# Moving the first job of the shared banks ahead of the keys in every slot of a one-core attention block

## The chip, the core and the metric

The kernel runs on one core of a Trainium2 chip. What counts is the device time of one execution, in microseconds (us). Three runs of the kernel before took 1745.03, 1745.07 and 1747.44 us; their median is 1745.07 us. One more execution was profiled, and all rows in this document come from it. The engines are named as in the profile: PE is TensorE (matmuls), PEld its weight loads, DVE VectorE, ACT ScalarE, POOL GpSimd, SP the engine that issues the DMAs.

## The reference, cut to what is computed

The batch is 32 sequences of 64 positions with width 512. Attention has 32 heads of width 128; a mask and a bias for each head and batch are added to the scores.

```python
xn  = layernorm(x)
q   = xn  @ Wq                 # (32*64, 32 heads, 128)
k   = ctx @ Wk ; v = ctx @ Wv
s   = q k^T * 128**-0.5 + bias # per batch and head, 64 x 64
p   = softmax(where(mask, s, -inf)), masked places 0
x   = x + tanh(g_xattn) * ((p v) @ Wo)
y   = layernorm(x)
x   = x + tanh(g_ffn) * (y @ Wf^T + bias + lora(y, adapter of the batch))
```

Everything is float32. The kernel keeps each matmul operand in two parts, `hi` (the value rounded) and `lo` (what the rounding left), and forms a product from three matmuls: hi·hi, hi·lo, lo·hi.

## The kernel before, in words

**Slots.** The 2048 rows are cut into 4 blocks of 512. A slot is one head of one block, so there are 128 slots, numbered n = 0 to 127; block b holds slots 32b to 32b+31. In a slot PE computes the queries of head n into `q_bank` (12 matmuls, `queries`), the keys into `k_bank` (12, `keys`), two jobs in the shared banks `vo_bank0/1` (`main_job(n, 0)` and `main_job(n, 1)`, 12 matmuls each), the scores of head n into `s_two` (8) and the attention of head n-1 into `pv_two` (8).

**Jobs of the shared banks.** Four heads make a group, and the two jobs of a slot go by n modulo 4. Slots 3 and 0 (modulo 4) compute values for a group (`values`), slots 1 and 2 compute the output projection of a finished group (`output`). The first output job of a group, in slot 1 (modulo 4), waits for `ot_lo`, the lo part of the attention result of the group's last head; that head's attention ran on PE at the end of the slot just before. Some slots carry more behind the two jobs: a `turn` (4 transposes of a normalised tile, in slots 9, 10, 13, 14 of blocks 1 to 3 and 25, 26, 29, 30 of blocks 0 to 2), a LoRA product (15, 16) or a piece of the dense layer (17 to 20, and the last slot of all).

**The other engines.** Each has a written list per slot and works it off in order. After the scores of a head DVE adds the bias and finds `row_max`; POOL subtracts it (`shift`); ACT takes the exponential; DVE sums rows and inverts; POOL scales (`probabilities`); DVE transposes through `pv_two` (`transposes`); ACT rounds to `pt` hi; DVE forms `pt` lo (`rest_of_probabilities`). That serves the attention of the next slot. The attention result goes ACT `attn`, DVE `attn` (the sum), ACT `ot_hi`, POOL `ot_lo`. A key tile goes ACT `kt` (hi), DVE `kt` (lo); a value tile ACT `v_hi`, DVE `v_lo`; an output job is added into `acc` by DVE.

**Weights.** Blocks 1 to 3 read weights back from DRAM already split. In block 0 they are split on the way: ACT makes the hi part (`weights_q`, `weights_vo`, `weights_k`), POOL the lo part of `wq`, `wk` and `wv`, DVE that of `wo` (`weights_o`, one piece before the transposes and one after, in slots 3 and 0 modulo 4). SP saves the split weights and loads the next raw ones, each in list order: in a slot it waits for `wq` lo, then for `wk` lo, then loads the raw pair for `wv` or `wo`.

Lines of the profile that the steps below touch: L296 to L298 are the three matmuls of a product, L301/L302 those of scores and attention, L575 the transposes of a turn, L679 every rounding on ACT, L743 ACT's half of `attn`, L737 `pt` hi, L858 every lo part on DVE, L887 the addition into `acc`, L903/L908 the transposes of the probabilities, L915 `pt` lo, L928/L933 scores and row maximum, L937 the attention sum, L965 the normalised tile, L1112 every lo part on POOL.

Of the kernel before, what the change touches and what calls it, by code (L numbers as in the profile page):

```python
# [163 lines left out]
def flamingo_block(nc, x, ctxt, pair_bias, mask, wq, wk, wv, wo, g_xattn, g_ffn, wf, fbias, lora_a, lora_b,  # L164
                   lora_starts, lora_const, out):
    with ExitStack() as ctx:
# [99 lines left out]
        def parts(pair, *at):  # L266
            return [p[at] for p in pair]
# [198 lines left out]
        def _(pe):  # L466
            def queries(n):
                b = n // H
                if n % H == 0:
                    pe.wait_ge(vo_free, NUMBER["turn", LEAD, b, PB - 1] + 1)  # L470
                if n < H:
                    pe.wait_ge(wq_lo, n + 1)
                else:
                    pe.wait_ge(wq_back, 16 * (n - H + 1))
                wait(pe, q_lo, n)
                for c in range(C):
                    mm = mm3(pe, q_bank[:, :], parts(q_w, slice(None), c, slice(None)),
                             parts(xt[b % 2], slice(None), c, slice(None)), c == 0, c == C - 1)
                mm.then_inc(q_ps, 1)

            def keys(n):
                b = n // H
                if n < H:
                    pe.wait_ge(wk_lo, n + 1)
                else:
                    pe.wait_ge(wk_back, 16 * (n - H + 1))
                wait(pe, k_lo, n)
                for c in range(C):
                    mm = mm3(pe, k_bank[:, :], parts(k_w, slice(None), c, slice(None)),
                             parts(ct[b % 2], slice(None), c, slice(None)), c == 0, c == C - 1)  # L490
                mm.then_inc(k_ps, 1)
# [53 lines left out]
            def main_job(n, k):  # L545
                if values_at(n):
                    g, tiles = values_at(n)
                    values(g, tiles[k])
                elif output_at(n):
                    g, tiles = output_at(n)  # L550
                    output(g, tiles[k])
# [55 lines left out]

            def slot(n):
                queries(n)
                keys(n)  # L610
                main_job(n, 0)
                main_job(n, 1)
                if turn_at(n):
                    turn(*turn_at(n))
                if lora_at(n):
                    lora_inner(*lora_at(n))
                if dense_at(n):
                    dense(*dense_at(n))
                scores(n)
                attention(n - 1)  # L620
# [56 lines left out]
        def _(act):  # L677
# [36 lines left out]
            def keys(n):  # L714
                wait(act, s_ps, n)
                act.wait_ge(k_ps, n + 1)
                hi(k_part(0), by(k_bank, PB), k_hi)
# [7 lines left out]
            def main_job(n, k):  # L725
                if values_at(n):
                    g, tiles = values_at(n)
                    values(g, tiles[k])

            def probabilities(n):  # L730
                if n == 0:
                    act.wait_ge(pt_zero, PB)
                wait(act, pv_ps, n)
                act.wait_ge(turn_done, n + 1)
                for r in range(2):
                    rows = cols(r, S)
                    last = act.activation(pt[rows, :, 0, rows], turned[rows, :, :], ACT.Copy)  # L737
                last.then_inc(pt_hi, 1)
# [40 lines left out]
            def slot(n):  # L779
                if n > 0:  # L780
                    queries(n)
                if n + 1 < H:
                    weights_q(n + 1)
                weights_vo(n)
                if n > 0:
                    keys(n)
                if n + 1 < H:
                    weights_k(n + 1)
                if n > 0:
                    probabilities(n - 1)  # L790
                if piece_at(n):
                    piece(n)
                if n > 0:
                    main_job(n, 0)
                    main_job(n, 1)
                if turn_at(n):
                    turn(*turn_at(n))
                if lora_at(n):
                    lora(*lora_at(n))
                if n > 0:  # L800
                    attention_half(n - 1)
                exps(n)
                if n > 0:
                    attention(n - 1)
# [51 lines left out]
        def _(dve):  # L856
# [7 lines left out]
            def keys(n):  # L864
                dve.wait_ge(k_hi, n + 1)
                lo(k_part(1), by(k_bank, PB), k_part(0), k_lo)
# [31 lines left out]
            def transposes(n):  # L898

                if n == 0:  # L900
                    dve.wait_ge(vo_free, NUMBER["v", 0, PB - 1] + 1)
                dve.wait_ge(prob_done, n + 1)
                dve.transpose(turned[:, :, :], prob[:, :, :]).then_inc(square_done, 1)  # L903
                dve.wait_ge(square_done, n + 1)
                for a in range(2):
                    for i in range(2):
                        of, to = cols(2 * a + i, S // 2), cols(2 * a + 1 - i, S // 2)
                        last = dve.transpose(turned[to, :, cols(i, S // 2)], prob[of, :, cols(1 - i, S // 2)])  # L908
                last.then_inc(turn_done, 1)

            def rest_of_probabilities(n):
                dve.wait_ge(pt_hi, n + 1)
                for r in range(2):
                    rows = cols(r, S)
                    last = dve.tensor_tensor(pt[rows, :, 1, rows], turned[rows, :, :], f32(pt[rows, :, 0, rows]),  # L915
                                             ALU.subtract)
                last.then_inc(pt_lo, 1)
# [102 lines left out]
            def slot(n):  # L1020
                if n > 0:
                    queries(n)
                    weights_o(n, 0)
                    transposes(n - 1)
                    keys(n)
                    rest_of_probabilities(n - 1)
                    weights_o(n, 1)
                if sums_at(n):
                    statistics(*sums_at(n))
                if turn_at(n):  # L1030
                    normalise(*turn_at(n))
                if n > 0:
                    main_job(n, 0)
                    main_job(n, 1)
                if turn_at(n):
                    turn(*turn_at(n))
                if lora_at(n):
                    lora_gate(*lora_at(n))
                if dense_at(n):
                    dense(*dense_at(n))  # L1040
                scores(n)
                if n > 0:
                    attention(n - 1)
                if lora_at(n):
                    lora_rest(*lora_at(n))
                row_scales(n)
                if n in CONSTANTS:
                    constants(CONSTANTS.index(n))
# [221 lines left out]
```

## Time and profile before

| | |
|---|---|
| median of three runs | 1745.07 us |
| the profiled execution | 1747.61 us, its span 1745.8 us |
| PE busy | 1726.5 us of the span, in 8666 matmuls |
| DVE, ACT, POOL busy | 1232.4, 619.3, 613.6 us |
| granted TensorE clock, mean | 0.997 |
| DMA | 336.50 MB, mean 193 GB/s; 281 to 215 GB/s in block 0, mostly 160 to 200 later |

The span is one execution from the first to the last instruction; 1.8 us of the execution lie outside it. PE's busy time is above 90% in all but the first and last of 40 slices, so the order of PE's own list sets the time, and another engine matters only where PE waits for it.

### The profile page before, as it was taken

Reading aid. Unit: us, or ns where it says so; the run is one execution under the profiler, and the core shown is the slowest. Engines: PE = TensorE matmul, PEld = TensorE weight load, DVE = VectorE, ACT = ScalarE, POOL = GpSimd, SP = SyncE. Lnnn points to the kernel's source line nnn. Section 1 sums busy time; section 2 is a strip of 40 time slices with the busy share of each in tenths; the row PEclk is TensorE's granted clock in tenths of the full one; section 3 lists DMA queues with packets and bytes.
Section 4 is the critical chain, followed back from the end, with each engine's and each line's share of the span. In section 5 each row is a group of like instructions: output and inputs, shape, how many; then the busy total and the mean of one; then the engine's idle time right before and its main releaser. Section 6 shows DMA issues by size and latency. Waiting matters only on the chain.

```text
span 1745.8 us, 25078 instructions
## 1 busy us (share of the span) xinstructions
PE 1726.5 (99%) x8666; PEld 1464.7 (84%) x8666; DVE 1232.4 (71%) x2649; ACT 619.3 (35%) x1225; POOL 613.6 (35%) x811
## 2 busy tenths in 40 slices
PE   8999999999999999999999999999999999999998
PEld 6888888888888888888888888888888888888887
DVE  6788777877777765667767776567766777666674
ACT  4544444454333332233333333223333333333321
POOL 4656666554232321233233232223332322222221
PEclk9999999999999999999999999999999999999999
DMA  7777777766545444555445454355455454454431
GB/s 281 266 260 257 280 262 273 279 233 215 183 169 199 170 163 159 192 174 200 163 167 195 167 193 171 134 200 192 164 184 178 170 197 159 159 193 162 177 125 49
DMA packets 111456, 336.50 MB, mean 193 GB/s; under 512 B 13361, under 2 KB 13489, under 8 KB 111330
## 3 DMA queue, kind: packets, MB, share of 16 engines
q1 hardware_dynamic: 111186, 334.63, 54.2%
q8 instruction: 70, 1.15, 0.3%
q14 instruction: 56, 0.46, 0.1%
q10 hardware_dynamic: 144, 0.26, 0.1%
HBM read 263.54 MB, written 71.30 MB: 192 GB/s over the span
## 4 chain that ended last, share of the span: by engine, by line
PE 95%; DVE 1%; issue 1%; POOL 1%; DMA 1%; ACT 0%; SPq 0%; ACTq 0%; DVEq 0%
PE vo_bank L296 13%; PE vo_bank L298 13%; PE vo_bank L297 13%; PE q_bank L296 7%; PE q_bank L298 7%; PE q_bank L297 7%; PE k_bank L296 6%; PE k_bank L297 6%; PE k_bank L298 6%; PE pv_two L301 5%; PE s_two L301 5%; PE pv_two L302 2%; PE s_two L302 2%; PE vo_bank L575 1%; DMA acc<-in_wv 0%
## 5 line engine op out<-in xcount | busy, mean ns | idle before, releaser
L1169 POOL TENSOR_TENSOR score<-score,row_max 128x256 f32<-128x256 f32 x128 | 78.8, 616 | 813.5 <-DVE row_max L933 813.5
L1112 POOL TENSOR_TENSOR ot_lo<-attn,ot_hi 128x512 fp32r<-128x512 f32 x128 | 165.7, 1294 | 151.5 <-ACT ot_hi L679 151.5
L296 PE MATMUL q_bank<-xt_hi,wq 128*128 128x512 f32 x512 | 209.0, 408 | 0.0
L298 PE MATMUL q_bank<-xt_hi,wq 128*128 128x512 f32 x512 | 201.0, 393 | 0.0
L297 PE MATMUL q_bank<-xt_lo,wq 128*128 128x512 f32 x512 | 200.4, 391 | 0.0
L296 PE MATMUL k_bank<-ct_hi,wk 128*128 128x512 f32 x512 | 199.3, 389 | 0.5 <-DVE ct_lo L858 0.5
L298 PE MATMUL k_bank<-ct_hi,wk 128*128 128x512 f32 x512 | 199.2, 389 | 0.0
L297 PE MATMUL k_bank<-ct_lo,wk 128*128 128x512 f32 x512 | 199.2, 389 | 0.0
L296 PE MATMUL vo_bank<-wv,ct_hi 128*128 128x512 f32 x504 | 196.3, 390 | 0.3 <-POOL wv L1112 0.3
L297 PE MATMUL vo_bank<-wv,ct_hi 128*128 128x512 f32 x504 | 196.1, 389 | 0.0
L298 PE MATMUL vo_bank<-wv,ct_lo 128*128 128x512 f32 x504 | 196.1, 389 | 0.0
L296 PE MATMUL vo_bank<-wo,ot_hi 128*128 128x512 f32 x496 | 193.2, 390 | 0.3 <-POOL ot_lo L1112 0.2
L298 PE MATMUL vo_bank<-wo,ot_lo 128*128 128x512 f32 x496 | 193.1, 389 | 0.0
L297 PE MATMUL vo_bank<-wo,ot_hi 128*128 128x512 f32 x496 | 193.0, 389 | 0.0
L743 ACT ACTIVATE attn<-pv_two 128x512 f32<-128x512 f32 x128 | 76.7, 599 | 318.8 <-PE pv_two L302 318.8
L908 DVE STREAM_TRANSPOSE pv_two<-prob 32x128 f32<-32x128 f32 x512 | 165.3, 323 | 9.6
L737 ACT ACTIVATE pt<-pv_two 64x256 fp32r<-64x256 f32 x256 | 97.0, 379 | 161.6 <-DVE pv_two L908 160.1
L858 DVE TENSOR_TENSOR v_lo<-vo_bank,v_hi 128x512 fp32r<-128x512 f32 x126 | 86.4, 691 | 89.4 <-ACT v_hi L679 88.1
L903 DVE STREAM_TRANSPOSE pv_two<-prob 128x256 f32<-128x256 f32 x128 | 58.9, 460 | 119.0 <-POOL prob L1183 118.7
L679 ACT ACTIVATE kt<-k_bank 128x512 fp32r<-128x512 f32 x128 | 76.6, 598 | 181.1 <-PE k_bank L298 180.4
L301 PE MATMUL s_two<-kt,qt_hi 128*128 128x256 f32 x512 | 127.8, 327 | 5.6 <-issue 5.6
L301 PE MATMUL pv_two<-pt,v_hi 128*128 128x256 f32 x512 | 132.9, 337 | 0.2 <-issue 0.2
(200 smaller groups left out, 3748.1 us busy)
## 6 DMA issues: line engine op xcount, KB each, us to landing
wv<-wv_split SPq DMA_DIRECT2D x96, 512.0 KB, 5.3
wq<-wq_split SPq DMA_DIRECT2D x96, 512.0 KB, 3.2
wk<-wk_split SPq DMA_DIRECT2D x96, 512.0 KB, 3.6
wo<-wo_split SPq DMA_DIRECT2D x96, 512.0 KB, 5.2
raw_bias<-in_pair_bias SPq DMA_DIRECT2D x64, 256.0 KB, 5.8
wq_split<-wq SPq DMA_DIRECT2D x32, 512.0 KB, 2.9
wk_split<-wk SPq DMA_DIRECT2D x32, 512.0 KB, 4.1
wv_split<-wv SPq DMA_DIRECT2D x32, 512.0 KB, 5.9
```

Source lines behind the costliest of these rows:

```text
L296: pe.matmul(to, left[0], right[0], start=first, stop=False)
L297: pe.matmul(to, left[0], right[1], start=False, stop=False)
L298: return pe.matmul(to, left[1], right[0], start=False, stop=last)
L301: pe.matmul(to, left[0], right, start=True, stop=False)
L302: return pe.matmul(to[:, 0, :], left[1], right[:, 0], start=False, stop=True)
L679: act.activation(to, src, func).then_inc(done, 1)
L737: last = act.activation(pt[rows, :, 0, rows], turned[rows, :, :], ACT.Copy)
L743: act.activation(by(attn, PB), pv_two[:, :, 1, :], ACT.Copy).then_inc(ot_b, 1)
L858: dve.tensor_tensor(to, src, f32(of), ALU.subtract).then_inc(done, 1)
L908: last = dve.transpose(turned[to, :, cols(i, S // 2)], prob[of, :, cols(1 - i, S // 2)])
L1112: pool.tensor_tensor(to, src, f32(of), ALU.subtract).then_inc(done, 1)
L1169: pool.tensor_tensor(score[:, :, :], score[:, :, :], row_max[:, :].unsqueeze(2).to_broadcast([P, PB, S]), ALU.subtract).then_inc(shift_don ...
```

## The change

Three lists are reordered; no instruction is added or removed. PE's slot becomes queries, first job, keys, second job, extras, scores, attention. ACT's list takes `probabilities` (the `pt` rounding) and the first job before `keys`; in block 0 the rounding of `wk` still follows `keys`. DVE's list takes `rest_of_probabilities`, the first job and the second piece of `weights_o` before `keys`. POOL's and SP's lists are as they were.

```diff
@@ PE
             def slot(n):
                 queries(n)
+                main_job(n, 0)
                 keys(n)
-                main_job(n, 0)
                 main_job(n, 1)
@@ ACT
                 weights_vo(n)
                 if n > 0:
+                    probabilities(n - 1)
+                    main_job(n, 0)
                     keys(n)
                 if n + 1 < H:
                     weights_k(n + 1)
-                if n > 0:
-                    probabilities(n - 1)
                 if piece_at(n):
                     piece(n)
                 if n > 0:
-                    main_job(n, 0)
                     main_job(n, 1)
@@ DVE
                     queries(n)
                     weights_o(n, 0)
                     transposes(n - 1)
+                    rest_of_probabilities(n - 1)
+                    main_job(n, 0)
+                    weights_o(n, 1)
                     keys(n)
-                    rest_of_probabilities(n - 1)
-                    weights_o(n, 1)
                 if sums_at(n):
                     statistics(*sums_at(n))
                 if turn_at(n):
                     normalise(*turn_at(n))
                 if n > 0:
-                    main_job(n, 0)
                     main_job(n, 1)
```

PE in slot 61 (block 1, 61 is 1 modulo 4, an output slot with a turn), before; of each product only rows that wait stand here:

```order
L296 MATMUL q_bank<-xt1_hi,wq 128x512 [waits q_lo,wq_back]
...
L296 MATMUL k_bank<-ct1_hi,wk 128x512 [waits k_lo,wk_back]
...
L296 MATMUL vo_bank0<-wo,ot1_hi 128x512 [waits vo_free,wo_back,ot_lo]
...
L296 MATMUL vo_bank1<-wo,ot1_hi 128x512 [waits vo_free]
...
L575 MATMUL vo_bank0<-ident,xn0 128x128 [waits vo_free,xn_done]
...
L301 MATMUL s_two<-kt,qt_hi 128x256 [waits score_done,k_lo,q_lo]
```

And the same rows now:

```order
L296 MATMUL q_bank<-xt1_hi,wq 128x512 [waits q_lo,wq_back]
...
L296 MATMUL vo_bank0<-wo,ot1_hi 128x512 [waits vo_free,wo_back,ot_lo]
...
L296 MATMUL k_bank<-ct1_hi,wk 128x512 [waits k_lo,wk_back]
...
L296 MATMUL vo_bank1<-wo,ot1_hi 128x512 [waits vo_free]
...
L575 MATMUL vo_bank0<-ident,xn0 128x128 [waits vo_free,xn_done]
...
L301 MATMUL s_two<-kt,qt_hi 128x256 [waits score_done,k_lo,q_lo]
```

The product that waits for `ot_lo` moved up by the 12 matmuls of the keys; the keys moved down by the 12 matmuls of that product.

DVE in slot 12 (block 0, 0 modulo 4, a value slot in which a second piece of `wo` is split), before, from the transposes on:

```order
L903 STREAM_TRANSPOSE pv_two<-prob 128x256 [waits prob_done]
L908 STREAM_TRANSPOSE pv_two<-prob 32x4x32 [waits square_done]
L908 STREAM_TRANSPOSE pv_two<-prob 32x4x32 x3
L858 TENSOR_TENSOR kt<-k_bank,kt 128x4x128 [waits k_hi]
L915 TENSOR_TENSOR pt<-pv_two,pt 64x4x64 [waits pt_hi]
L915 TENSOR_TENSOR pt<-pv_two,pt 64x4x64
L858 TENSOR_TENSOR wo<-raw_vo,wo 128x512 [waits wo_hi]
L858 TENSOR_TENSOR v_lo<-vo_bank,v_hi 128x2x256 [waits vo_hi] x2
```

And now (line numbers one lower, since the file is a line shorter):

```order
L902 STREAM_TRANSPOSE pv_two<-prob 128x256 [waits prob_done]
L907 STREAM_TRANSPOSE pv_two<-prob 32x4x32 [waits square_done]
L907 STREAM_TRANSPOSE pv_two<-prob 32x4x32 x3
L914 TENSOR_TENSOR pt<-pv_two,pt 64x4x64 [waits pt_hi]
L914 TENSOR_TENSOR pt<-pv_two,pt 64x4x64
L857 TENSOR_TENSOR v_lo<-vo_bank,v_hi 128x2x256 [waits vo_hi]
L857 TENSOR_TENSOR wo<-raw_vo,wo 128x512 [waits wo_hi]
L857 TENSOR_TENSOR kt<-k_bank,kt 128x4x128 [waits k_hi]
L857 TENSOR_TENSOR v_lo<-vo_bank,v_hi 128x2x256 [waits vo_hi]
```

`kt` lo, for which the scores wait, moved from before `pt` lo to behind `pt` lo, the first value tile and the piece of `wo`. In blocks 1 to 3 the row of `wo` is not there.

ACT in the same slot, before:

```order
L679 ACTIVATE wo<-raw_vo 128x512 [waits vo_ps,raw_vo_in1,wo_saved]
L679 ACTIVATE kt<-k_bank 128x4x128 [waits k_ps,s_ps]
L679 ACTIVATE wk<-raw_k 128x512 [waits wk_saved,k_ps,raw_k_in]
L737 ACTIVATE pt<-pv_two 64x4x64 [waits turn_done,pv_ps]
L737 ACTIVATE pt<-pv_two 64x4x64
L679 ACTIVATE v_hi<-vo_bank 128x2x256 [waits vo_ps,pv_ps] x2
```

And now:

```order
L679 ACTIVATE wo<-raw_vo 128x512 [waits vo_ps,raw_vo_in1,wo_saved]
L737 ACTIVATE pt<-pv_two 64x4x64 [waits turn_done,pv_ps]
L737 ACTIVATE pt<-pv_two 64x4x64
L679 ACTIVATE v_hi<-vo_bank 128x2x256 [waits vo_ps,pv_ps]
L679 ACTIVATE kt<-k_bank 128x4x128 [waits k_ps,s_ps]
L679 ACTIVATE wk<-raw_k 128x512 [waits wk_saved,k_ps,raw_k_in]
L679 ACTIVATE v_hi<-vo_bank 128x2x256 [waits vo_ps,pv_ps]
```

The roundings of `kt` and `wk` moved behind that of `pt` and of the first value tile.

## Rows read from the trace of the kernel before

**Rows 1.** Waits of PE: waited for, total us, times, longest us.
```profile
PE s_two L301 <- issue: 5.6, 2, 4.1
PE vo_bank L575 <- DVE acc L887: 4.4, 3, 1.9
```

**Rows 2.** Timeline of PE, slots 60 and 61: start us, us, instruction.
```profile
805.99 0.45 PE L296 MATMUL q_bank<-xt_hi,wq 128*128 128x512 f32 x1
...
816.95 0.28 PE L301 MATMUL s_two<-kt,qt_hi 128*128 128x256 f32 x1
...
818.75 0.45 PE L296 MATMUL q_bank<-xt_hi,wq 128*128 128x512 f32 x1
...
821.55 0.39 PE L296 MATMUL k_bank<-ct_hi,wk 128*128 128x512 f32 x1
...
824.27 0.39 PE L296 MATMUL vo_bank<-wo,ot_hi 128*128 128x512 f32 x1
```

**Rows 3.** Timeline of DVE, ACT and POOL from those scores to `ot_lo`.
```profile
817.84 0.69 DVE L858 TENSOR_TENSOR v_lo<-vo_bank,v_hi 128x512 fp32r<-128x512 f32 x1 [1.28 <-ACT v_hi L679]
...
820.67 0.69 DVE L937 TENSOR_TENSOR attn<-pv_two,attn 128x512 f32<-128x512 f32 x1
...
821.75 0.62 ACT L679 ACTIVATE ot_hi<-attn 128x512 fp32r<-128x512 f32 x1
...
822.45 1.29 POOL L1112 TENSOR_TENSOR ot_lo<-attn,ot_hi 128x512 fp32r<-128x512 f32 x1 [1.11 <-ACT ot_hi L679]
```

**Rows 4.** Timeline of POOL and PE, slot 25: its first output job.
```profile
336.53 1.30 POOL L1112 TENSOR_TENSOR ot_lo<-attn,ot_hi 128x512 fp32r<-128x512 f32 x1 [1.39 <-ACT ot_hi L679]
...
337.89 0.50 PE L296 MATMUL vo_bank<-wo,ot_hi 128*128 128x512 f32 x1 [0.19 <-POOL ot_lo L1112]
```

**Rows 5.** Timeline of DVE, slot 60: `kt` and `pt` lo.
```profile
813.72 0.69 DVE L858 TENSOR_TENSOR kt<-k_bank,kt 128x512 fp32r<-128x512 f32 x1
...
814.59 0.86 DVE L915 TENSOR_TENSOR pt<-pv_two,pt 64x256 fp32r<-64x256 f32 x2 [0.17 <-ACT pt L737]
```

**Rows 6.** Timeline of DVE and PE, slot 58, an output slot with a turn.
```profile
788.59 0.86 DVE L915 TENSOR_TENSOR pt<-pv_two,pt 64x256 fp32r<-64x256 f32 x2 [0.17 <-ACT pt L737]
789.48 0.55 DVE L965 TENSOR_SCALAR xn<-acc,mean_var,rstd 128x512 f32<-128x512 f32 x1
...
791.00 0.60 PE L575 MATMUL vo_bank<-ident,xn 128*128 128x128 f32 x4
```

**Rows 7.** Timeline of DVE and PE, slot 12 in block 0.
```profile
175.23 0.86 DVE L915 TENSOR_TENSOR pt<-pv_two,pt 64x256 fp32r<-64x256 f32 x2 [0.17 <-ACT pt L737]
...
176.12 0.69 DVE L858 TENSOR_TENSOR wo<-raw_vo,wo 128x512 fp32r<-128x512 f32 x1
...
177.09 0.28 PE L301 MATMUL s_two<-kt,qt_hi 128*128 128x256 f32 x1
```

**Rows 8.** Timeline of DVE and PE at the start (slot 1) and the end (slot 127).
```profile
37.65 0.86 DVE L915 TENSOR_TENSOR pt<-pv_two,pt 64x256 fp32r<-64x256 f32 x2 [0.48 <-ACT pt L737]
...
37.26 0.55 PE L301 MATMUL s_two<-kt,qt_hi 128*128 128x256 f32 x1 [4.05 <-issue]
...
1696.40 0.86 DVE L915 TENSOR_TENSOR pt<-pv_two,pt 64x256 fp32r<-64x256 f32 x2 [0.17 <-ACT pt L737]
...
1697.04 0.28 PE L301 MATMUL s_two<-kt,qt_hi 128*128 128x256 f32 x1
```

**Rows 9.** Timeline of PE and DVE around the turns of slots 25 and 57.
```profile
345.52 0.63 PE L575 MATMUL vo_bank<-ident,xn 128*128 128x128 f32 x4 [1.90 <-DVE acc L887]
...
774.91 1.29 DVE L952 BATCH_NORM_STATS2 stats<-acc 128x6 f32<-128x512 f32 x2
...
776.39 0.52 DVE L965 TENSOR_SCALAR xn<-acc,mean_var,rstd 128x512 f32<-128x512 f32 x1
...
777.78 0.63 PE L575 MATMUL vo_bank<-ident,xn 128*128 128x128 f32 x4 [1.23 <-DVE acc L887]
```

**Rows 10.** Windows of PE: stretch, length, PE busy (matmuls), granted clock, DMA, GB/s.
```profile
775.00:778.00 3.00, 1.77 (x9) 1.00 0.74 295
...
346.70:350.00 3.30, 3.30 (x15) 0.50 0.99 385
```

## The prediction

> **What bounds the kernel now.** I read the page first: PE is busy in nearly every slice, so its own list sets the time. The waits of PE come next [rows 1]: two waits before scores at the start (5.6 us) and three before turns (4.4 us) are nearly all. The timeline of a plain slot then gives the floor [rows 2]: queries begin at 805.99 and the next ones at 818.75, so a slot takes 12.76 us of unbroken PE work; queries are 2.80 us (818.75 to 821.55), 12 matmuls of keys or of a job 2.72 us (821.55 to 824.27). A reordering takes none of this away. It can gain only from the 10 us of waits, and it can lose wherever a product moves ahead of its operand. So each wait in PE's list has to be asked how late its operand comes. All times below are those of the profiled execution, 1747.61 us (span 1745.8 and 1.8 outside); the median of the runs lies 2.5 us lower.
>
> **The first output job of a group.** In 31 slots (5, 9, ... 125) the first job waits for `ot_lo` of the head whose attention PE finished just before the slot. In slot 61 the scores before it began at 816.95 [rows 2]; from there DVE sums at 820.67, ACT rounds at 821.75, POOL works 822.45 to 823.74 [rows 3]. That is 6.79 us after the scores. The job began 7.32 us after them (824.27), so 0.53 us was spare. In slot 25, where the chain was late, PE already waited, and began at 337.89, 0.06 us after POOL's end at 337.83 [rows 4]. The job now begins behind the queries alone: 821.55, 4.60 us after the scores, but `ot_lo` lets it go at 6.79 + 0.06 = 6.85. PE stands still 2.25 us, with the keys, the second job and the scores queued behind it. Nothing of this comes back, for neither DVE, ACT nor POOL can start that chain sooner: its parts hang on the scores and attention of the slot before.
>
> The chain is not the same everywhere. In front of it DVE has the second value tile of slot 60 (817.84 for 0.69 us, [rows 3]), which delays the scores' sums by 0.32 us. Where slot n-1 has a long PE tail (after LoRA and dense work: 49, 53, 81, 85, 113) that tile is done early and the wait is 1.93 us; the same holds in block 0, for a reason below. Blocks 1 to 3: 17 x 2.25 + 5 x 1.93 = 47.9 us, and slots 57 and 89 apart. There PE waits today before the turn, since DVE runs statistics and normalisation (774.91 to 776.91, [rows 9]) before the addition that frees the bank. The first job's bank is now freed before; but `kt` lo, which stands ahead of the statistics, comes late, as the keys end 6.85 + 5.44 + 0.17 = 12.46 us after the scores of slot 56. ACT's rounding (0.6) and DVE's (0.6 until the next can start) bring the statistics to 13.7, their 2.0 us and a hand-over of 0.1 the turn to 15.8, where it began 14.2 after those scores: 1.6 us each, 3.2 together. Sum 51.1.
>
> Block 0: five slots at 1.93 = 9.7, and slots 25 and 29, which already wait, 1.7 together. Sum 11.4.
>
> **The scores' wait for `kt` lo.** DVE used to form `kt` lo (813.72) while ACT rounded `pt`, so it cost nothing; then `pt` lo to 815.45 [rows 5], 1.50 us before the scores at 816.95. Now the value tile or addition (0.60 until the next may start) and `kt` lo (0.69) follow `pt` lo, with gaps of 0.03 and a hand-over of 0.10: 1.42 us. That is 0.08 less than the 1.50 there are: a plain slot costs nothing, but the cover is nearly gone. Bounds: 0 and, if the pieces run 0.13 longer each, 0.2 us in 24 slots, 5 us.
>
> In slots with a turn that are 2 modulo 4 (12 of them) the normalised tile also comes behind `kt` lo: 789.45 + 0.03 + 0.60 + 0.60 + 0.55 + 0.10 = 791.33 for a turn that began at 791.00 [rows 6]: 0.33 x 12 = 4.0 us. Those that are 1 modulo 4 are covered by the longer slot.
>
> In block 0, slots 0 and 3 modulo 4 also have a piece of `wo` (0.73) between. Slot 12: `pt` lo ends 176.09 [rows 7], less 0.32 (PE waited in slot 11 too, so the second value tile is out of the way before the scores; that is the reason named above), + 0.03 + 0.60 + 0.73 + 0.69 + 0.10 = 177.92 against scores at 177.09: 0.83 us. Other slots of the eight stand at 0.8 to 1.6; I take 1.05: 8.4 us. Slots 3 modulo 4 (seven from 7 on) come out at 0.85 to 1.6 by the same sum, and their raw `wo` arrives later, since SP asks for it only after POOL's `wk` and `wv` lo, which follow the keys' rounding on ACT. Bounds of that: 0, where the chain has other reasons to be late, and the 2.7 us by which the keys move; I take 0.4, near the lower end, as ACT needs the load only before it rounds `pt`: 7 x 1.4 = 9.8 us.
>
> Start: in slot 1 the scores wait for `kt` lo as it is (37.26), `pt` lo ending at 38.51 [rows 8]; with `pt` first, both scores waits grow by about 1, and slot 3 has two pieces of `wo` and a late load: 4.4 us in all, between 1 and 8. End: slot 127 has no job; `pt` lo ends at 1697.26, + 0.03 + 0.69 + 0.10 = 1698.08 against 1697.04 [rows 8]: 1.0 us.
>
> Sum without the clock: 51.1 + 11.4 + 4.0 + 8.4 + 9.8 + 4.4 + 1.0 = 90.1 us.
>
> **The clock.** After the 1.90 us of idle PE before the turn of slot 25 [rows 9] the granted clock fell to 0.50, that is 1.2 in place of 2.4 GHz, for about 3.4 us [rows 10], which costs half, 1.7 us. After 1.23 us idle in slot 57 [rows 9] it stayed at 1.00 [rows 10]. The 31 new waits leave PE idle 1.8 to 2.1 us (the wait less 0.17 us in which the last matmul drains), as long as the one after which it fell; but that one was followed by transposes and short matmuls, these by full ones. Bounds: none of them, 0, and all, 53 us. I take half of them, 15.5 x 1.7 = 26 us.
>
> The Trainium skill (TensorE: Matmul & The Clock Gate, section "HAM oscillation — how this bites in real kernels") has as its rule that only idle gaps longer than any of these let the clock fall. By that rule the 26 us would be 0. The trace does not agree: it fell after 1.90 us [rows 9, 10].
>
> Forecast: 1747.6 + 90.1 + 26 = 1863.7 for a profiled execution, 1861 for a run.
>
> **Rivals.**
> The clock holds in all new waits (the page's rule above would have it so): 1745.1 + 90.1 = 1835. For it: two of three waits near a turn left the clock alone. Against it: [rows 10].
> The clock falls in all of them: 1835 + 53 = 1888. For it: a fall after a shorter idle time. Against it: full matmuls before and after.
> The starved block 0: SP's later loads put ACT's rounding of `wo` ahead of `pt` by 2 us more in 14 slots, 28 us on top: 1889. Against it: ACT has nothing else to do between the queries' rounding and `pt`, so the load must be over 2 us late before it counts.
> The other side, not slower, is that the bank relief decides. Place: turns of slots 25, 57 and 89, where the addition that frees the bank now stands before the statistics. Price: the 4.4 us of waits [rows 1] and one spell at half clock, 1.7, so 1739. It decides only if the wait for `ot_lo` stays below 6 / 31 = 0.2 us, so only if POOL's part ended 4.7 us after the scores and not 6.79. Nothing in the rows shortens that chain by 2 us.
> The change not doing what it says is excluded by the order: the waiting product stands ahead of the keys.
>
> **How the numbers follow.** Some falls of the clock, 1848 to 1878: 0.45. No falls, 1825 to 1848: 0.25. All falls or the starved block, 1878 to 1905: 0.20. A smaller loss than any of these, 1750 to 1825 (half of the waits hidden by something I don't see): 0.05. Not slower, 1739: 0.03, and within 0.2%: 0.02. A change of 0.2% (3.5 us) is about what a measurement of this kernel can tell from none. Range 1825 to 1895: it leaves out 0.10 below and some 0.05 above.
>
> **What would show it.** Right: PE's waits have a new first line, the output job at L296 behind POOL's `ot_lo`, about 31 times and near 60 us; in a slot like 61 the job begins 6.85 us after the scores; scores wait in block 0 alone, 14 to 17 times and near 1 us; some 15 spells at clock 0.50 each behind such a wait; plain slots 60, 62 and 63 still take 12.76 us. Wrong: `ot_lo` ending earlier than 6.4 us after the scores, waits for `kt` in every slot of blocks 1 to 3, or a block 0 that grows by more than 50 us.

## The result and the profile after

The changed kernel takes 1853.11 us (median of four runs, 1848.67 to 1858.37); the kernel before, run beside it, takes 1745.05 (1744.06 to 1747.44). The ratio is 1.0613, with a 95% interval of 1.0599 to 1.0627: slower by 108 us. The forecast was 1861, range 1825 to 1895. The profiled execution spans 1846.8 us against 1745.8, 101.0 us more and not 108: it took 1848.67 us, the least of the four, and the profiled one of before took 1747.61, more than any of its four.

The page shows the same instructions in a longer span. First the busy times of the engines, then the chain that ended last:

```profile
PE 1753.6 (95%) x8666; PEld 1466.0 (79%) x8666; DVE 1217.3 (66%) x2649; ACT 612.1 (33%) x1225; POOL 617.5 (33%) x811
...
PE 80%; DVE 8%; POOL 4%; issue 4%; ACT 3%; DMA 1%; SPq 0%; ACTq 0%; DVEq 0%
```

PE was busy 99% and made up 95% of the chain; now it stands still for 5% of the span, and the chain leaves it for DVE, ACT and POOL. Its waits (waited for, total us, times, longest us), against [rows 1]:

```profile
PE vo_bank L296 <- POOL ot_lo L1111: 59.2, 31, 2.1
PE s_two L301 <- issue: 20.3, 18, 3.7
PE vo_bank L575 <- DVE xn L964: 3.4, 6, 1.4
```

The new first line is the output job behind POOL's `ot_lo`, in all 31 groups. The scores' waits grew from 5.6 us in 2 to 20.3 in 18 ("issue" stands there for `kt` lo, as the timelines below show): slots 1 and 2, the slots 0 and 3 modulo 4 from 3 to 32 but 31, and 127. The turn's wait for an addition on DVE is gone, but one for the normalised tile `xn` has come in its place, 1.4 us in slot 25 and 0.66 in 57 and 89, so little of it is won.

Slot 61 on PE, with the scores of slot 60 ahead of it (start us, us, instruction, idle time and releaser); it answers to [rows 2]:

```profile
867.77 0.28 PE L301 MATMUL s_two<-kt,qt_hi 128*128 128x256 f32 x1
...
874.58 0.50 PE L296 MATMUL vo_bank<-wo,ot_hi 128*128 128x512 f32 x1 [2.02 <-POOL ot_lo L1111]
874.92 0.40 PE L297 MATMUL vo_bank<-wo,ot_hi 128*128 128x512 f32 x1
...
877.48 0.39 PE L296 MATMUL k_bank<-ct_hi,wk 128*128 128x512 f32 x1
```

And the chain on DVE, ACT and POOL in that stretch, as in [rows 3]:

```profile
868.66 0.69 DVE L857 TENSOR_TENSOR v_lo<-vo_bank,v_hi 128x512 fp32r<-128x512 f32 x1 [1.08 <-ACT v_hi L679]
...
871.49 0.69 DVE L936 TENSOR_TENSOR attn<-pv_two,attn 128x512 f32<-128x512 f32 x1
...
872.57 0.61 ACT L679 ACTIVATE ot_hi<-attn 128x512 fp32r<-128x512 f32 x1
...
873.26 1.27 POOL L1111 TENSOR_TENSOR ot_lo<-attn,ot_hi 128x512 fp32r<-128x512 f32 x1 [1.11 <-ACT ot_hi L679]
```

The chain is as long as before: `ot_lo` ends at 874.53, 6.76 us after the scores (6.79 before). The queries end 4.6 us after them, and PE goes on at 874.58, 6.81 after them; 6.85 was forecast. One thing was not: the second matmul of the job starts 0.34 us after the first, where matmuls in a row follow at 0.23 (0.31 to 0.34 over the 31 waits), so each such wait costs 0.1 us on top of the idle time.

Where each part of a period (scores to scores) changed, after less before, read slot by slot from the two traces:

| group of slots | forecast | measured |
| --- | --- | --- |
| 1 modulo 4, blocks 1 to 3 (24), without the clock | 51.1 | 53.4 |
| 1 modulo 4, block 0 (7) | 11.4 | 13.8 |
| 2 modulo 4 with a turn (12) | 4.0 | 3.6 |
| 0 modulo 4, slots 4 to 32 (8) | 8.4 | 7.1 |
| 3 modulo 4 from slot 7 on, block 0 (7) | 9.8 | 9.2 |
| up to the scores of slot 3 | 4.4 | 2.1 |
| slot 127 | 1.0 | 1.05 |
| half-clock spells behind the new waits | 26 | 11.4 |
| slot 26: a half-clock spell of before is gone | - | -1.1 |
| all others | 0 | 0.4 |
| sum | 116 | 101.0 |

One entry has another cause than the rest of its row. In slot 31 PE waits not for `kt` lo but for the DMA that brings `wv` back, since the first job, which needs it, comes sooner (neither the kernel before nor that of experiment 10, with the old order in this slot, has the wait):

```profile
PE vo_bank L296 <- DMA wv<-wv_split: 1.3, 1, 1.3
```

### The profile page after: what moved, and what is told of

Its sections match the earlier page's. It is cut to its first block, busy times and chain, and to the rows that moved or that the text cites. A ratio compares the mean times of both kernels' runs of the same rounds, so it can differ in the third digit from the quotient of the medians.

```text
span 1846.8 us, 25078 instructions
## 1 busy us (share of the span) xinstructions
PE 1753.6 (95%) x8666; PEld 1466.0 (79%) x8666; DVE 1217.3 (66%) x2649; ACT 612.1 (33%) x1225; POOL 617.5 (33%) x811
## 4 chain that ended last, share of the span: by engine, by line
PE 80%; DVE 8%; POOL 4%; issue 4%; ACT 3%; DMA 1%; SPq 0%; ACTq 0%; DVEq 0%
PE vo_bank L296 13%; PE vo_bank L297 12%; PE vo_bank L298 12%; PE k_bank L296 6%; PE k_bank L297 6%; PE k_bank L298 6%; PE q_bank L296 5%; PE q_bank L298 5%; PE q_bank L297 5%; PE s_two L301 4%; DVE score L927 4%; PE pv_two L301 3%; POOL ot_lo L1111 2%; ACT ot_hi L679 2%; PE s_two L302 1%
## 5 line engine op out<-in xcount | busy, mean ns | idle before, releaser
L296 PE MATMUL vo_bank<-wo,ot_hi 128*128 128x512 f32 x496 | 201.0, 405 | 59.2 <-POOL ot_lo L1111 59.2
L297 PE MATMUL vo_bank<-wo,ot_hi 128*128 128x512 f32 x496 | 197.9, 399 | 0.0
L298 PE MATMUL vo_bank<-wo,ot_lo 128*128 128x512 f32 x496 | 197.5, 398 | 0.0
L914 DVE TENSOR_TENSOR pt<-pv_two,pt 64x256 fp32r<-64x256 f32 x256 | 108.1, 422 | 116.6 <-ACT pt L737 114.9
L296 PEld LDWEIGHTS vo_bank<-wo,ot_hi 128*128 128x128 f32 x496 | 95.2, 192 | 91.8 <-POOL ot_lo L1111 72.3
L301 PE MATMUL s_two<-kt,qt_hi 128*128 128x256 f32 x512 | 128.7, 329 | 20.3 <-issue 20.3
```

The lines of the kernel that those rows point to most:

```text
L296: pe.matmul(to, left[0], right[0], start=first, stop=False)
L297: pe.matmul(to, left[0], right[1], start=False, stop=False)
L298: return pe.matmul(to, left[1], right[0], start=False, stop=last)
L301: pe.matmul(to, left[0], right, start=True, stop=False)
```

## The experiments

All twelve are built from the two kernels. Ratios are against the kernel before, run beside them on the same chip (medians 1747.6, 1748.2 and 1746.8 us), with 95% intervals. "A spell" is a stretch in which full matmuls follow each other at 0.43 us in place of 0.23.

**1. Old order in the slots with the waits.** The changed kernel with the order of before in slots 1 modulo 4, on PE, ACT and DVE. The edit on PE (ACT and DVE alike):

```diff
 queries(n)
-main_job(n, 0)
-keys(n)
+if n % G == 1:
+    keys(n); main_job(n, 0)
+else:
+    main_job(n, 0); keys(n)
```

> The changed kernel, with the old order (keys before the first job) put back on PE, ACT and DVE in the slots that are 1 modulo 4 alone. Theory (the attention result's lo part is late): all 31 waits for ot_lo go, 53 us of them in blocks 1 to 3, 14 in block 0 and the 11 us of half clock behind them, so 1853 - 78 = 1775 us. Rival (the new order costs in every slot, through kt lo or the banks, and the wait on ot_lo only shows it): the time then moves into the other slots, and stays above 1820 us.

Measured: 1771.96 us, ratio 1.0151 (1.0125 to 1.0177); the forecast of 1775 held, the rival (over 1820) did not. In its profile the slots 1 modulo 4 of blocks 1 to 3 are within 0.1 us of before in sum, and no spell is left but those at the start, up to slot 3. What remains is block 0 (6.9 us in slots 0 modulo 4, 7.7 in slots 3 modulo 4), the turns of slots 2 modulo 4 (3.7), the start and the end. So of the 108 us, 84 go when the 31 slots are put back (80 by the two profiles), and 24 stay.

**2 and 3. The wait, pushed back.** In the changed kernel the first output job waits for the last head's `ot_lo` only ahead of that head's three matmuls (2), or after the first head's three (3), its first matmuls needing only the earlier heads:

```diff
-pe.wait_ge(ot_lo, G * (g + 1))
+pe.wait_ge(ot_lo, G * (g + 1) - 1)
 ...
-output_heads(g, t, range(G))
+output_heads(g, t, range(3))       # range(1) in the other kernel
+pe.wait_ge(ot_lo, G * (g + 1))
+output_heads(g, t, range(3, G))    # range(1, G)
```

> The changed kernel, with the first output job's wait split: its first three heads (9 of 12 matmuls) wait only for the heads before, the last three matmuls for ot_lo of the last head. Theory: 9 x 0.2265 = 2.04 of each wait of 2.25 us are filled with work, 31 x 2.04 = 63 us and the 11 us of half clock go, some 4 us come back as waits before turns: about 1783 us. Rival (the keys behind the job are what is late, or the banks): nothing is gained by splitting, 1853 us.

> As the split after three heads, but after one: 3 x 0.2265 = 0.68 us of each wait filled, idle time per wait about 1.4 us in place of 2.1. Theory for the waits: 31 x 0.68 = 21 us less. For the clock: if falls hang on the length of the idle time, there are none behind these waits and another 11 us go: 1821 us. Rival: the clock falls as often as before, 7 times: 1832 us.

Measured: 1779.54 us, ratio 1.019 (1.0169 to 1.021), for the first, where 1783 was forecast: the wait is gone, no output job is followed by a spell, and 74 of the 108 us are saved. The second: 1819.26 us, ratio 1.0418 (1.0398 to 1.0438). Its wait of PE:

```profile
PE vo_bank L296 <- POOL ot_lo L1116: 37.5, 31, 1.4
```

Thirty-one waits are there still, 1.0 to 1.4 us each, and none of them is followed by a spell. The forecast of 1821 held, its rival of 1832 (spells as before) did not. So it is not enough for a spell that there is such a wait; among these waits its length matters.

**4. The new PE order only where the wait is.** The kernel before, with PE's first job ahead of the keys in slots 1 modulo 4; ACT and DVE as before:

```diff
 queries(n)
+if n % G == 1:
+    main_job(n, 0)
 keys(n)
-main_job(n, 0)
+if n % G != 1:
+    main_job(n, 0)
 main_job(n, 1)
```

> The kernel before, with the new order in the slots that are 1 modulo 4 on PE alone; ACT's and DVE's lists are the old ones everywhere. Theory: the 31 waits for ot_lo are there, 53 + 12 us, with some falls of the clock (0 to 15 us), and nothing of block 0's waits for kt lo: 1745 + 65 + 8 = 1818 us. Rival (loss spread over all slots): under 1775 us.

Measured: 1866.33 us, ratio 1.0687 (1.0668 to 1.0707). The forecast missed by 48 us. Its waits of PE:

```profile
PE vo_bank L296 <- POOL ot_lo L1115: 63.9, 31, 2.9
PE vo_bank L575 <- DVE acc L890: 17.6, 12, 3.5
```

The second line has grown from 4.4 us in 3 before: 12 turns wait for the addition that frees their bank. And 18 of the 31 waits are followed by a spell, where the changed kernel has 7. Block 0's slots 0 and 3 modulo 4 are as before, as expected.

**5. The piece of `wo` behind the keys on DVE.** The changed kernel, block 0:

```diff
 main_job(n, 0)
-weights_o(n, 1)
 keys(n)
+weights_o(n, 1)
```

> The changed kernel, with the second piece of wo (block 0, slots 0 and 3 modulo 4) behind the keys on DVE in place of before them. Theory: each of the 15 waits for kt lo in block 0 gets 0.73 us shorter, 11 us: 1842 us. Rival (they wait for SP's late raw weights or ACT): no change, 1853 us.

Measured: 1855.28 us, ratio 1.0611 (1.0588 to 1.0634), as the changed kernel; 1842 was forecast, a miss. First slot 12 in the changed kernel, which answers to [rows 7], then in this one (DVE, POOL and PE in both):

```profile
186.67 0.86 DVE L914 TENSOR_TENSOR pt<-pv_two,pt 64x256 fp32r<-64x256 f32 x2 [0.90 <-ACT pt L737]
...
188.17 0.68 DVE L857 TENSOR_TENSOR wo<-raw_vo,wo 128x512 fp32r<-128x512 f32 x1
188.34 1.64 POOL L1111 TENSOR_TENSOR wk<-raw_k,wk 128x512 fp32r<-128x512 f32 x1 [2.50 <-ACT wk L679]
188.76 0.68 DVE L857 TENSOR_TENSOR kt<-k_bank,kt 128x512 fp32r<-128x512 f32 x1
189.55 0.36 PE L301 MATMUL s_two<-kt,qt_hi 128*128 128x256 f32 x1 [0.50 <-issue]
...
192.57 0.42 DVE L932 TENSOR_REDUCE row_max<-score 128x4 f32<-128x256 f32 x1
```

```profile
187.65 0.68 DVE L857 TENSOR_TENSOR kt<-k_bank,kt 128x512 fp32r<-128x512 f32 x1
187.83 1.27 POOL L1111 TENSOR_TENSOR wk<-raw_k,wk 128x512 fp32r<-128x512 f32 x1 [2.49 <-ACT wk L679]
188.25 1.40 DVE L857 TENSOR_TENSOR wo<-raw_vo,wo 128x512 fp32r<-128x512 f32 x1
188.43 0.36 PE L301 MATMUL s_two<-kt,qt_hi 128*128 128x256 f32 x1 [0.43 <-issue]
189.57 0.68 DVE L857 TENSOR_TENSOR v_lo<-vo_bank,v_hi 128x512 fp32r<-128x512 f32 x1
...
191.94 0.42 DVE L932 TENSOR_REDUCE row_max<-score 128x4 f32<-128x256 f32 x1
```

The first shows the forecast's order: `pt` lo, value tile, `wo`, `kt` lo, and the scores 0.11 us behind `kt` lo. In the second `kt` lo no longer stands behind `wo`, yet the scores' wait is shorter by 0.07 only. `wo` now delays the work behind it: `row_max` starts 3.51 us after the scores in place of 3.02.

The two profiles show where the forecast 11 us went. The fifteen waits of the scores got shorter, but by 3.6 us in sum. The seven waits for `ot_lo` of block 0 got longer by 3.1 us in sum (about 2.2 us each in place of 1.7), and those of slots 9, 21 and 25 are now followed by a spell, where none was. That the later `row_max` is what makes these waits longer, and keeps the scores' waits from shrinking by the full 0.73 us each, is likely, since an item moved along DVE's list stands in the way of another there, but no run shows it by itself.

`wo` took 1.40 us here, and 0.68 in the changed kernel, though POOL works on `wk` beside it in both. What differs is who began. Here POOL did (187.83): it took 1.27 us, and `wo` ended 0.55 us after it (188.25 + 1.40 against 187.83 + 1.27). In the changed kernel `wo` began 0.17 us ahead of POOL, and it was POOL that took longer, 1.64 us. With POOL idle `wo` took 0.69 us in all 12 such cases of the kernel before. The value tile and `kt`, which DVE reads from PSUM on one side, kept their 0.68 or 0.69 beside POOL. This agrees with the Trainium skill (SBUF — State Buffer, section "Who interferes with whom"), by which a DVE instruction with both inputs in SBUF contends with a POOL instruction that reads SBUF, over a port pair that only one of them can hold.

**6 and 7. PE's list alone.** The kernel before with PE's new order in all slots and the old lists on ACT and DVE; and the same with the wait pushed back as in 2:

```diff
 queries(n)
-keys(n)
 main_job(n, 0)
+keys(n)
 main_job(n, 1)
```

> PE's list as in the changed kernel, ACT's and DVE's as before (kt ahead of pt). Theory: kt lo then waits only for the keys themselves, which end 10.2 us after the scores, and is ready at 11.5, 1.2 us before the next scores; block 0's 17 us of waits for kt lo go, those for ot_lo stay: 1853 - 17 = 1836 us. pt lo then ends at 12.5, 1 us before the attention. Rival (the lists have to match, since pt and the first job now wait behind kt on ACT and DVE): slower than 1853 us.

> PE's list as in the changed kernel with the split after three heads, ACT's and DVE's lists as before. Theory: both late operands are covered; left are 31 x 0.2, some 5 us of waits before turns and the start: 1745 + 6 + 5 + 3 = 1759 us. Rival (the new order has no cost but these, and takes the bank waits of slots 25, 57 and 89 away): 1742 us.

Measured: 1896.99 us, ratio 1.0858 (1.0843 to 1.0873), and 1812.05 us, ratio 1.0364 (1.035 to 1.0378). Both forecasts (1836, 1759) missed. For 6 the rival was right (the lists have to match: slower than 1853); for 7 its rival, 1742, was further off than the forecast. The waits of PE in the first, then ACT, DVE and PE at the turn of slot 61:

```profile
PE vo_bank L296 <- POOL ot_lo L1112: 70.0, 31, 4.5
PE vo_bank L575 <- DVE acc L887: 31.0, 24, 3.5
```

```profile
910.86 0.60 ACT L679 ACTIVATE kt<-k_bank 128x512 fp32r<-128x512 f32 x1 [8.35 <-PE k_bank L298]
...
911.49 0.69 DVE L858 TENSOR_TENSOR kt<-k_bank,kt 128x512 fp32r<-128x512 f32 x1 [5.42 <-ACT kt L679]
912.14 0.86 DVE L915 TENSOR_TENSOR pt<-pv_two,pt 64x256 fp32r<-64x256 f32 x2
913.03 0.55 DVE L965 TENSOR_SCALAR xn<-acc,mean_var,rstd 128x512 f32<-128x512 f32 x1
913.61 1.29 DVE L887 TENSOR_TENSOR acc<-vo_bank,acc 128x512 f32<-128x512 f32 x2
914.45 0.63 PE L575 MATMUL vo_bank<-ident,xn 128*128 128x128 f32 x4 [0.97 <-DVE acc L887]
```

ACT and DVE wait for keys that PE now computes last (8.35 and 5.42 us idle), while the first job, long done, stands behind `kt`, `pt` and `xn`. Its addition starts at 913.61 and holds the bank until 914.3; the turn waits 0.97 us. This is a wait that the changed lists of ACT and DVE save, and the reason of the 17.6 us in 4 as well: there too only PE's list had changed. It is not the whole of the 44 us between 6 and the changed kernel. The waits for `ot_lo` are 11 us longer (70.0 against 59.2) and 19 of them are followed by a spell in place of 7, while the scores wait 16 us less (3.9 against 20.3).

**8. A cheaper start of three turns.** The kernel before; on DVE, where statistics and a turn meet (slots 25, 57, 89), the normalised tile and the first addition go ahead of the statistics:

```diff
-if sums_at(n): statistics(*sums_at(n))
+both_here = bool(sums_at(n) and turn_at(n))
+if sums_at(n) and not both_here: statistics(*sums_at(n))
 if turn_at(n): normalise(*turn_at(n))
-if n > 0: main_job(n, 0); main_job(n, 1)
+if n > 0: main_job(n, 0)
+if both_here: statistics(*sums_at(n))
+if n > 0: main_job(n, 1)
```

> The kernel before, where a slot has both statistics and a turn (25, 57, 89): DVE takes the normalised tile and the first job's addition ahead of the statistics, which serve a later tile. PE's list is the old one. Theory: the three waits before these turns (1.90, 1.23, 1.23 us idle) and the one spell at half clock (1.7 us) go, 0.6 us come back by the later scores: 1745 - 5.5 = 1739.5 us, ratio 0.997. Rival (the turn then waits for the tile, the scores for DVE): within 1 us of 1745.

Measured: 1744.12 us in 9 runs against 1748.2 in 13, ratio 0.9975 (0.9965 to 0.9985): faster than both kernels, by 4.1 us against the kernel before where 5.5 were forecast. The periods of slots 57 and 89 are 1.42 us shorter, that of 25 by 1.3, the spell behind it is gone (0.65 us in slot 26), and slots 58 and 90 give back 0.4 each. The turn of slot 57 on DVE and PE, against [rows 9]:

```profile
775.14 0.55 DVE L965 TENSOR_SCALAR xn<-acc,mean_var,rstd 128x512 f32<-128x512 f32 x1
775.72 0.69 DVE L887 TENSOR_TENSOR acc<-vo_bank,acc 128x512 f32<-128x512 f32 x1
776.33 1.28 DVE L952 BATCH_NORM_STATS2 stats<-acc 128x6 f32<-128x512 f32 x2
776.62 0.60 PE L575 MATMUL vo_bank<-ident,xn 128*128 128x128 f32 x4
```

The bank is free at 776.4, ahead of PE, and the 1.23 us of idle time are gone.

**9. The same, with the keys first in slot 1 on ACT.**

```diff
 queries(n)
+if n == 1: keys(n)
 weights_q(n + 1)
+if n == 1: probabilities(0)
 weights_vo(n)
-keys(n)
+if n > 1: keys(n)
 ...
-probabilities(n - 1)
+if n > 1: probabilities(n - 1)
```

> This kernel is e8_before_norm_first (the order of the kernel before, with the normalised tile and the first job ahead of the statistics in slots 25, 57 and 89) with one edit more, on ACT in slot 1 alone: the rounding of the keys and of the probabilities stands ahead of the roundings of the weights of head 2. The trace of before shows the scores of slots 1 to 3 waiting 5.6 us in all for the keys' low part, because the keys' rounding stands behind a whole set of weight roundings. Theory: that ring is what makes PE wait in slot 1, the scores of slot 1 come about 3 us sooner, and since PE then runs without a pause the 3 us stay: about 1741 us, ratio 0.996 or a little less. Rival: the weights of head 2, now rounded some 1.5 us later on ACT and so later on POOL, make the queries or keys of slot 2 wait as long: 1744, same as e8. If the ring is closed elsewhere (DVE), also 1744.

Measured: 1743.77 us in 11 runs, ratio 0.9981 (0.9972 to 0.999). The intervals of 8 and 9 overlap, so no gain over 8 can be told; the rival stands. Slot 1's wait fell from 4.1 us to 1.7, and the scores of slot 2 then waited 2.9 in place of 1.5:

```profile
34.51 0.35 PE L301 MATMUL s_two<-kt,qt_hi 128*128 128x256 f32 x1 [1.69 <-issue]
...
46.74 0.35 PE L301 MATMUL s_two<-kt,qt_hi 128*128 128x256 f32 x1 [2.93 <-issue]
```

Right behind the first of these waits the clock fell to 0.50, after 1.69 us of idle PE. The window (length, PE busy, granted clock, DMA, GB/s):

```profile
35.40:38.50 3.10, 3.05 (x13) 0.50 0.70 232
```

In experiment 8 it fell in slot 2, from 51.8 us on, behind idle times of 1.52 and 0.23 us ahead of the scores and the attention.

**10. The complement of 1.** The kernel before with the new order in slots 1 modulo 4 on all three engines. On PE as in 4; on DVE (ACT likewise):

```diff
 transposes(n - 1)
-keys(n)
-rest_of_probabilities(n - 1)
-weights_o(n, 1)
+if n % G == 1:
+    rest_of_probabilities(n - 1); main_job(n, 0); weights_o(n, 1); keys(n)
+else:
+    keys(n); rest_of_probabilities(n - 1); weights_o(n, 1)
 ...
-if n > 0: main_job(n, 0)
+if n > 0 and n % G != 1: main_job(n, 0)
```

> The order of the kernel before everywhere, except in slots 1 modulo 4, where PE, ACT and DVE all have the new order (first job ahead of the keys). It is the complement of e1 (old order only in those slots, 1772, so 26 us of the 108 were outside them) and differs from e4 (1866) only in that the ACT and DVE lists go along. Theory: the effects are local to a slot; the wait for the attention's low part (24 slots of 2.3 in blocks 1 to 3, 7 of 2.0 in block 0, about 67 us) and the half-clock spells behind it, 11 us, come back, the waits of e4 for the turn's bank do not: 1745 + 53 + 14 + 11 = about 1824, with 5 to 10 spells. Rival: the turns' wait and the more frequent spells of e4 come from the mixture of slots and not from its lists: 1850 or more, some 20 spells. A second rival for the clock alone: 1824 + 15 if some 20 of 31 waits are followed by a spell whatever the lists are.

Measured: 1841.47 us, ratio 1.0537 (1.0518 to 1.0556). The forecast of 1824 fell short by the clock, as its second rival had it:

```profile
PE vo_bank L296 <- POOL ot_lo L1126: 63.9, 31, 2.9
...
PE vo_bank L575 <- DVE acc L894: 0.3, 1, 0.3
```

The wait for `ot_lo` is that of 4 to the last digit, and the turns no longer wait for additions: the 17.6 us of 4 came from the lists that had not been changed. But 17 of the 31 waits are followed by a spell, so the many spells of 4 did not come from there. The other slots of blocks 1 to 3 are within 0.1 us of before in sum. Experiments 1 and 10 add up to 24 + 95 = 119 us for a change that costs 108. The excess of 11 is less than ten more spells at 1.6 us; without spells the slots 1 modulo 4 of blocks 1 to 3 cost 53.6 here and 53.4 in the changed kernel.

**11 and 12. Is a spell chance?** The changed kernel and the kernel of 10, each profiled once more, with no edit.

> The changed kernel itself, profiled a second time, for its half-clock spells alone. In its first profile 7 of the 31 waits for the attention's low part (slots 37, 41, 73, 105, 117, 121, 125) were followed by a spell at half clock. Theory: whether the clock falls behind a wait of about 2 us differs from one execution to the next; then the waits are the same to 0.1 us, but the spells stand behind other slots and their number may be anything from 3 to 12, with the span moving by 1.6 us for each. Rival: the program decides it, by what stands around each wait; then the same seven slots, and a span within 1 us of 1846.8.

> The kernel of e10_new_order_output1_all a second time, again for its spells. There some 17 of 31 waits were followed by one. Theory of chance in each execution: other slots, between 10 and 22 of them. Rival, the program decides: the same slots and a span within 1 us of 1843.6. If both are half right (the mean is the program's, the slots are chance), this one keeps a clearly larger number than the changed kernel in e11, over 12 against under 12.

Measured: spans 1851.3 and 1838.7 us. In 11 the waits followed by a spell are those of slots 37, 41, 73, 105, 117, 121 and 125: the same seven. Experiment 5 shows these seven in blocks 1 to 3 too. In 12 there are 15, of which 14 are among the 17 of experiment 10. So the rival was right nearly throughout as to the slots: the program settles, but for a few, which waits are followed by a spell. It was wrong as to the spans, which it had within 1 us. That of 11 is 4.5 us longer, and 4.4 of that lies ahead of the scores of slot 3: what differs between these executions is the start. That of 12 is 4.9 us shorter, with two spells fewer and 1.0 us less ahead of slot 3's scores.

## Why the forecast held, point by point

**The number.** It came out 8 us above the median of the runs, and 15 above the profiled execution (1863.7 against 1848.67), which is the one that the terms can be held against. The clock's term was 14.6 us too high and the start's 2.3, the waits for `ot_lo` 4.7 too low, and a spell of before that went away (1.1) had no term. The mechanisms were right; that the number came so near is in part these errors working against each other, and the waits and spells below are the better measure. Two signs named ahead were missed: some 15 spells (7), and scores that wait in block 0 alone, 14 to 17 times (18, with slots 32 and 127 among them).

**The bound.** Right. PE's list sets the time, and the slots in which no operand moved (blocks 1 to 3, all but 1 modulo 4 and the turns) changed by 0.4 us in sum over 60 slots (slot 32 stands with block 0, 127 apart).

**The first output job.** Right. The chain kept its length, and 31 waits came out at 59.2 us idle. The term is 64.8 + 13.8 - 11.4 = 67.2 without the clock against 62.5 forecast. The difference is the 0.1 us behind each wait (31 x 0.1 = 3.1), which no row of before had shown apart, and slots 25 and 29, 3.2 us together where 1.7 stood. Slots 57 and 89 came out at 1.8 and 1.6, forecast at 1.6. Experiment 1 shows the cause by taking the order back, experiment 2 by taking only the wait away.

**The scores' wait for `kt` lo.** Right. In plain slots the forecast left 0.08 us of cover; slot 60 took 12.77 us, and here are its `pt`, value and key tiles on DVE, against [rows 5], with the scores at 867.77 right behind:

```profile
865.40 0.86 DVE L914 TENSOR_TENSOR pt<-pv_two,pt 64x256 fp32r<-64x256 f32 x2 [0.90 <-ACT pt L737]
866.29 0.69 DVE L857 TENSOR_TENSOR v_lo<-vo_bank,v_hi 128x512 fp32r<-128x512 f32 x1
866.90 0.68 DVE L857 TENSOR_TENSOR kt<-k_bank,kt 128x512 fp32r<-128x512 f32 x1
```

`kt` ends at 867.58, 0.19 us ahead of the scores, of which 0.11 is the hand-over seen in slot 12: 0.08 spare, as forecast. Slots 2 modulo 4 with a turn grew by 0.31 to 0.35 us each but slot 30, by 0.44 (0.33 forecast); block 0 cost 16.3 against 18.2. The bound of 2.7 us for a late load of `wo` was never reached. The last slot, as in [rows 8]:

```profile
1797.20 0.69 DVE L857 TENSOR_TENSOR kt<-k_bank,kt 128x512 fp32r<-128x512 f32 x1
...
1798.00 0.36 PE L301 MATMUL s_two<-kt,qt_hi 128*128 128x256 f32 x1 [0.89 <-issue]
```

**The start.** Its size can't be judged: 2.1 us in the first profile and 6.5 in the second, where 4.4 was forecast. Two executions of one kernel differ here by as much as the term.

**The clock.** The mechanism is right, the term is the one mis-sized: 11.4 us against 26. Slot 37 on PE, then the windows of its stretches and of the same stretch in slot 61 (length, PE busy, granted clock, DMA, GB/s), against [rows 10]:

```profile
530.56 0.50 PE L296 MATMUL vo_bank<-wo,ot_hi 128*128 128x512 f32 x1 [2.02 <-POOL ot_lo L1111]
530.90 0.39 PE L297 MATMUL vo_bank<-wo,ot_hi 128*128 128x512 f32 x1
...
532.33 0.63 PE L296 MATMUL vo_bank<-wo,ot_hi 128*128 128x512 f32 x1
532.76 0.63 PE L297 MATMUL vo_bank<-wo,ot_hi 128*128 128x512 f32 x1
```

```profile
530.60:531.90 1.30, 1.30 (x5) 0.93 0.41 164
531.95:534.85 2.90, 2.90 (x8) 0.50 0.00 0
...
874.60:878.00 3.40, 3.40 (x15) 1.00 0.19 74
```

After 2.02 us of idle PE the first matmuls still run at full clock, and the fall comes while the fifth runs (from 531.7 us on); then seven or eight follow each other at 0.43 us (1.2 in place of 2.4 GHz), which costs 1.6 us. In slot 61, behind the same 2.02 us, nothing falls. The forecast put one price on all 31 waits, with half of them to fall. But 13 of them were 1.8 us or less (block 0 but slot 25, slots behind a long PE tail, 33 and 89), and the clock fell behind none of these; behind the 18 of 2.0 us and more it fell 7 times. Over the nine profiles here with such waits (two of them second executions of a kernel), 0 of 90 waits for `ot_lo` of 1.8 us or less were followed by a spell, and 95 of 166 of 2.0 us or more. That is no bound for other waits: ahead of scores the clock fell behind 1.69 us (experiment 9). With the count of long waits and the forecast's own half the term would have been 9 x 1.6 = 14. Which long waits are followed by a spell is settled by the program but for a few (experiments 11 and 12); what in it settles that stays open. In blocks 1 to 3 the changed kernel has 7 of 17, that of experiment 10 has 11 of 19, with the same order in these slots and idle times that differ by 0.03 us.

The rule of the Trainium skill that the forecast weighed (TensorE: Matmul & The Clock Gate, section "HAM oscillation — how this bites in real kernels") would have let no such wait count. The runs do not agree: seven spells stand behind some 2.0 us of idle time in the changed kernel.

**The rivals.** The clock holding throughout (1835) and falling throughout (1888) were both off, the first by less. The starved block 0 did not come. The relief of the bank is real, as the changed kernel has no wait of that kind, but the turns of slots 25, 57 and 89 then wait for the normalised tile; experiment 8 has the relief by itself, with 1744.12 us. It is small beside the waits, as the forecast said.

## What to carry to other kernels

On an engine that is full, a reordering costs what the moved item's operand is late by, and that can be read in advance: the end of the last link of its chain against the end of what now stands ahead of it, here to 0.05 us. Where one engine's list is reordered, the lists of the engines that free its buffers have to follow, or a second wait appears (experiment 6 against the changed kernel: 44 us, spells and longer first waits included; experiment 7 against 2, with the first wait gone or nearly so: 33). If a late operand can't be avoided, wait for it ahead of the part that reads it, not ahead of the whole product: experiment 2 took back 74 of 108 us with that alone.

## What the runs showed of the hardware that was not expected

- The clock of PE fell behind 95 of the 166 waits for `ot_lo` of 2.0 us or more and behind none of the 90 of 1.8 us or less, but ahead of scores it fell behind 1.69 us. In a second execution it fell behind the same seven of the 18 long waits in one kernel, and in another behind 15, of which 14 were among the 17 of the first.
- The first matmul after a wait for `ot_lo` holds the next back: 0.31 to 0.34 us from start to start in place of 0.23.
- DVE's subtraction of two tiles in SBUF took 0.69 us with POOL idle. Where POOL's subtraction had begun first, DVE's ended 0.55 us after it and so took 1.40; where DVE's had begun first it kept its 0.68, and POOL's took 1.64 in place of 1.27. With one input in PSUM DVE's took 0.68 or 0.69 beside POOL.
